# Decoder layer on one core: the feed-forward stage as a written-out pipeline, gate and up in two bank pairs that ScalarE empties

## The reference

```python
def mx_linear(x, w):
    return jnp.einsum('bsh,oh->bso', mx_qdq(x), mx_qdq(w))
g = mx_linear(x, w_gate)
u = mx_linear(x, w_up)
return mx_linear(jax.nn.silu(g) * u, w_down)
...
x = _layernorm(x + _L0_ffn_ref(x, L0_ffn_w_gate, L0_ffn_w_up, L0_ffn_w_down), axis=-1)
```

## Time and profile before

| | |
|---|---|
| median of 3 runs | 887.55 us (886.04 to 888.01) |
| profiled execution | 885.64 us, span 883.8 us |
| busy share of the span | PE 78%, VectorE 73%, ScalarE 59%, POOL 54% |
| granted PE clock, mean | 0.92 of full speed |
| attention pipeline, 300 to 600 us | PE busy 100 of each 100 us, VectorE 83 to 86 |
| feed-forward stage, 750 to 800 us | of 50 us: PE 38.84, VectorE 34.12, ScalarE 15.83, POOL 24.53; clock 0.93 |

### The profile page before, as it was taken

How to read it: one execution, slowest core, us unless ns; L and a number is a source line. 1 busy time by engine, 2 the same in 40 slices (tenths; PEclk the granted TensorE clock), 3 DMA queues, 4 the chain that set the end, 5 groups by cost and what they waited for, 6 DMA issues and landing times.

```text
span 883.8 us, 15272 instructions
## 1 busy us (share of the span) xinstructions
PE 689.3 (78%) x5249; PEld 380.0 (43%) x5264; DVE 642.4 (73%) x1236; ACT 524.6 (59%) x953; POOL 480.7 (54%) x538
## 2 busy tenths in 40 slices
PE   2024665655899999999999999999985787777774
PEld 2013554552345544445444554445552343333331
DVE  4566877775877888888889888898723676667663
ACT  1127878764678777787777877778752233333321
POOL 4223333331647776677766777767653344444452
PEclk9999767676899999999999999999996999999996
DMA  8996101110000000000000000000000000000000
GB/s 197 233 196 216 37 24 36 35 43 1 12 13 1 13 13 14 13 1 13 13 14 13 7 7 13 14 13 1 1 1 0 1 24 24 24 24 24 24 23 26
DMA packets 25829, 30.91 MB, mean 35 GB/s; under 512 B 4016, under 2 KB 16304, under 8 KB 25776
## 3 DMA queue, kind: packets, MB, share of 16 engines
q1 hardware_dynamic: 25776, 30.22, 12.8%
HBM read 26.02 MB, written 4.19 MB: 34 GB/s over the span
## 4 chain that ended last, share of the span: by engine, by line
PE 55%; DVE 11%; POOL 11%; issue 10%; ACT 7%; DMA 4%; ACTq 1%; SPq 1%; POOLq 0%; DVEq 0%
PE banks L1207 7%; PE banks L1168 7%; PE banks L1197 7%; PE banks L1219 7%; PE banks L1178 7%; PE banks L1242 6%; PE banks L1133 6%; ACT big L831 5%; POOL big L544 4%; DVE big L561 4%; POOL rstd L539 3%; DMA big<-in_L_ffn_w_down_dram 2%; DVE big L796 2%; PE banks L1257 2%; DMA big<-in_L_ffn_w_up_dram 2%
## 5 line engine op out<-in xcount | busy, mean ns | idle before, releaser
L831 ACT ACTIVATE big<-banks 128x512 f32<-128x512 f32 (+3 forms) x352 | 197.0, 593 | 73.8 <-PE banks L1197 43.5
L475 POOL TENSOR_TENSOR big<-big 128x512 f32<-128x512 f32 x128 | 131.6, 1049 | 4.3 <-DVE big L697 4.3
L677 DVE TENSOR_REDUCE big<-banks 128x1 f32<-128x512 f32 x128 | 83.0, 681 | 49.7 <-PE banks L1168 48.5
L467 POOL TENSOR_TENSOR big<-big 128x512 f32<-128x512 f32 x64 | 81.2, 1269 | 56.2 <-ACT big L918 56.2
L1133 PE MATMUL banks<-big 128*128 128x128 f32 x256 | 57.8, 417 | 53.7 <-ACT big L831 53.7
L831 ACT ACTIVATE big<-big 32x256 f32<-32x256 f32 (+4 forms) x112 | 90.4, 835 | 1.1
L544 POOL TENSOR_TENSOR big<-big 128x1376 f32<-128x1376 f32 x16 | 40.1, 2508 | 92.4 <-DVE big L565 92.4
L913 ACT ACTIVATE big<-banks,big 128x512 f32<-128x512 f32 x128 | 87.2, 682 | 3.9 <-DVE big L677 3.7
L1047 ACT ACTIVATE big<-big,shift,rstd 128x512 f32<-128x512 f32 x16 | 13.0, 812 | 124.4 <-POOL shift L540 124.4
L683 DVE TENSOR_REDUCE big<-banks 128x16 f32<-128x1024 f32 x64 | 76.6, 1198 | 9.6 <-PE banks L1178 9.6
L918 ACT ACTIVATE big<-big 128x1024 f32<-128x1024 f32 x64 | 67.2, 1050 | 21.9 <-DVE big L688 21.9
(11 more groups left out here) (104 smaller groups left out, 1220.7 us busy)
## 6 DMA issues: line engine op xcount, KB each, us to landing
big<-in_x_dram SPq DMA_DIRECT2D x2, 2048.0 KB, 16.7
big<-in_x_dram SPq DMA_DIRECT2D x4, 1024.0 KB, 10.2
xt<-in_x_dram SPq DMA_DIRECT2D x1, 4096.0 KB, 14.9
big<-in_ctx_dram SPq DMA_DIRECT2D x16, 256.0 KB, 2.8
out_dram<-big SPq DMA_DIRECT2D x16, 256.0 KB, 2.0
big<-in_L_ffn_w_down_dram SPq DMA_DIRECT2D x4, 688.0 KB, 6.9
big<-in_L_ffn_w_gate_dram SPq DMA_DIRECT2D x10, 256.0 KB, 2.6
big<-in_L_ffn_w_up_dram SPq DMA_DIRECT2D x10, 256.0 KB, 2.7
```

The costliest lines, as they stand in the source:

```text
L475: pool.tensor_tensor(e, e, r, ALU.mult).then_inc(s.p_ready, 1)
L677: dve.tensor_reduce(kneg[:, par, i:i + 1], bank[par], X, ALU.max, negate=True).then_inc(s.k_max_ready, 1)
L831: return act.activation(dst, src, ACT.Copy)
```

## The change

The feed-forward stage becomes a pipeline written out tile by tile on every engine, without loops, with more tiles in flight. Gate and up of a chunk go to a pair of banks (0 and 1, or 2 and 3, alternating by chunk). ScalarE empties both: silu of gate into `hs`, which has three slots, and a copy of up into the new `us`, which has two. VectorE multiplies `hs` by `us` in place in one operation of 1376 columns (`multiply_h`), and POOL scales in place too (`shift_hidden`). `hk`, `hq`, `hqT`, `yo`, `xo` and the columns of the output norm have two slots; the down product alternates between banks 6 and 7, in two parts of six and five pieces; all transposes, of x and of h, share banks 4 and 5. Storing uses two semaphores. The last tiles of the attention pipeline are written out, and the first gate and up chunk stands ahead of the last tile's `spread_rn` on PE. The diff, cut:

```diff
...
+        hs = cut(3 * FFN).rearrange("p (s n) -> p s n", s=3)
+        us = cut(2 * FFN).rearrange("p (s n) -> p s n", s=2)
         h8 = cut(FFN // 4).bitcast(FP8)
-        hq = cut(FFN // 2).bitcast(BF16)
-        hqT = cut(FT * P // 2).bitcast(BF16).rearrange("p (f t) -> p f t", f=FT)
-        xqT = cut(L).bitcast(BF16).rearrange("p (s k t) -> p s k t", s=2, k=KT)
-        yo = cut(L)
-        xo = cut(L)
-        hk = [cut(GH) for _ in range(3)]
+        hk = [[cut(GH) for _ in range(3)] for _ in range(2)]
+        assert off <= 4 * NJ * L
+
+        off = 4 * NJ * L
+        hq = cut(FFN).bitcast(BF16).rearrange("p (s n) -> p s n", s=2)
+        hqT = cut(FT * P).bitcast(BF16).rearrange("p (s f t) -> p s f t", s=2, f=FT)
+        yo = cut(2 * L).rearrange("p (s n) -> p s n", s=2)
+        xo = cut(2 * L).rearrange("p (s n) -> p s n", s=2)
...
-            with sp.Fori(0, T) as t:
-                sp.wait_ge(s.out_ready, t + 1)
-                sp.dma_start(out_tok[t], xo).then_inc(s.out_stored, 16)
-            sp.wait_ge(s.out_stored, 16 * T)
+            for u in range(T):
+                sp.wait_ge(s.out_ready, u + 1)
+                sp.dma_start(out_tok[u], xo[:, u % 2]).then_inc(s.out_stored[u % 2], 16)
...
+            def shift_hidden(u):
+                pool.wait_ge(s.h_inv_ready, u + 1)
+                h = hs[:, u % 3]
+                pool.tensor_tensor(groups(h), groups(h), spread(hk[u % 2][1], GH), ALU.mult).then_inc(s.hy_ready, 1)
+
+            def out_rsqrt(u):
+                k = u % 2
+                pool.wait_ge(s.ln_var, u + 1)
+                if u >= 2:
+                    pool.wait_ge(s.out_ready, u - 1)
+                pool.tensor_tensor(neg_mean_o[:, k:k + 1], zero[:], mv_o[:, k, 0:1], ALU.subtract)
+                ch.link(pool.tensor_tensor(vare[:], mv_o[:, k, 1:2], eps_tile[:], ALU.add))
+                ch.link(pool.tensor_tensor(rstd_o[:, k:k + 1], vare[:], minus_half[:, 0:1], ALU.pow))
+                pool.tensor_tensor(shift_o[:, k:k + 1], neg_mean_o[:, k:k + 1], rstd_o[:, k:k + 1], ALU.mult
+                                   ).then_inc(s.ln_shift, 1)
+
+            for f in range(-1, T + 1):
...
+            rsqrt_y(T - 1)
+            add_y(T - 1)
+            x2_rsqrt(T - 1)
+            shift_x(T - 1)
+            for u in range(0, T + 4):
+                if u - 4 in tiles:
+                    out_rsqrt(u - 4)
+                if u in tiles:
+                    shift_hidden(u)
...
+            def multiply_h(u):
+                dve.wait_ge(s.silu_ready, NC * u + NC)
+                dve.wait_ge(s.u_copied, NC * u + NC)
+                dve.tensor_tensor(hs[:, u % 3], hs[:, u % 3], us[:, u % 2], ALU.mult).then_inc(s.h_ready, 1)
+
+            def scale_hidden(u):
+                dve.wait_ge(s.h_ready, u + 1)
+                if u >= 2:
+                    dve.wait_ge(s.hy_ready, u - 1)
+                group_scales(hs[:, u % 3], *hk[u % 2]).then_inc(s.h_inv_ready, 1)
+
+            def clip_hidden(u):
+                dve.wait_ge(s.hy_ready, u + 1)
+                to_fp8(h8, hs[:, u % 3]).then_inc(s.h_clipped, 1)
+
+            def dequant_hidden(u):
+                dve.wait_ge(s.h_clipped, u + 1)
+                if u >= 2:
+                    dve.wait_ge(s.tr_ready, tr_no[u - 2, "h1"] + 1)
+                else:
+                    dve.wait_ge(s.tr_ready, tr_no[T - 1, "p13"] + 1)
+                dve.tensor_tensor(groups(hq[:, u % 2]), groups(h8), spread(hk[u % 2][2], GH), ALU.mult
+                                  ).then_inc(s.hq_ready, 1)
+
+            def add_down(u):
+                dve.wait_ge(s.down_part, 2 * u + 2)
+                if u >= 2:
+                    dve.wait_ge(s.out_ready, u - 1)
+                dve.tensor_tensor(yo[:, u % 2], xt[:, u], bank[6 + u % 2], ALU.add).then_inc(s.down_added, 1)
+
+            def out_stats(u):
+                dve.wait_ge(s.down_added, u + 1)
+                if u >= 2:
+                    dve.wait_ge(s.ln_shift, u - 1)
+                ch.link(dve.bn_stats(st6[:], yo[:, u % 2]))
+                dve.bn_aggr(mv_o[:, u % 2], st6[:]).then_inc(s.ln_var, 1)
...
+            x2_stats(T - 1)
+            scale_x(T - 1)
+            quantize_x(T - 1)
+            for u in range(1, T + 5):
+                if u - 2 in tiles:
+                    scale_hidden(u - 2)
+                if u - 3 in tiles:
+                    clip_hidden(u - 3)
+                    dequant_hidden(u - 3)
+                if u - 5 in tiles:
+                    add_down(u - 5)
+                    out_stats(u - 5)
+                if u - 1 in tiles:
+                    multiply_h(u - 1)
...
+            def silu(u, c):
+                c0, w = CH[c]
+                m = NC * u + c
+                act.wait_ge(s.gu_ready, m + 1)
+                if u >= 3:
+                    act.wait_ge(s.h_clipped, u - 2)
+                act.activation(hs[:, u % 3, c0:c0 + w], bank[2 * (m % 2)][:, 0:w], ACT.Silu).then_inc(s.silu_ready, 1)
+
+            def copy_u(u, c):
+                c0, w = CH[c]
+                m = NC * u + c
+                act.wait_ge(s.gu_ready, m + 1)
+                if u >= 2:
+                    act.wait_ge(s.h_ready, u - 1)
+                copy(us[:, u % 2, c0:c0 + w], bank[2 * (m % 2) + 1][:, 0:w]).then_inc(s.u_copied, 1)
...
+            def result(u):
+                k = u % 2
+                act.wait_ge(s.ln_shift, u + 1)
+                if u >= 2:
+                    act.wait_ge(s.out_stored[k], 16 * (u // 2))
...
+            norm_x2(T - 2)
+            bias_y(T - 1)
+            copy_xT(0)
+            silu(0, 0)
+            copy_u(0, 0)
+            silu(0, 1)
+            copy_u(0, 1)
+            copy_xT(1)
+            silu(0, 2)
+            norm_x2(T - 1)
+            copy_u(0, 2)
+            silu(1, 0)
+            copy_u(1, 0)
+            silu(1, 1)
+            copy_u(1, 1)
+            for u in range(2, T + 6):
+                if u in tiles:
+                    copy_xT(u)
+                if u - 1 in tiles:
+                    silu(u - 1, 2)
+                    copy_u(u - 1, 2)
+                if u - 6 in tiles:
+                    result(u - 6)
+                if u in tiles:
+                    silu(u, 0)
+                    copy_u(u, 0)
+                if u - 3 in tiles:
+                    copy_h(u - 3, 0)
+                if u in tiles:
+                    silu(u, 1)
+                if u - 3 in tiles:
+                    copy_h(u - 3, 1)
+                if u in tiles:
+                    copy_u(u, 1)
...
+            def gate_up(u, c):
+                c0, w = CH[c]
+                m = NC * u + c
+                if c == 0:
+                    pe.wait_ge(s.tr_copied, tr_no[u, "x"] + 1)
+                if m == 0:
+                    pe.wait_ge(s.k_exp_done, 8 * T)
+                elif m == 1:
+                    pe.wait_ge(s.q_shifted, 4 * T)
+                else:
+                    pe.wait_ge(s.silu_ready, m - 1)
+                    pe.wait_ge(s.u_copied, m - 1)
+                for o, wT in ((bank[2 * (m % 2)], wgT), (bank[2 * (m % 2) + 1], wuT)):
+                    for f in range(KT):
+                        last = pe.matmul(o[:, 0:w], xqT[:, u % 2, f], wT[:, f, c0:c0 + w],
+                                         start=(f == 0), stop=(f == KT - 1))
+                last.then_inc(s.gu_ready, 1)
...
+            y_product(T - 1, 0)
+            y_product(T - 1, 1)
+            y_product(T - 1, 2)
+            y_product(T - 1, 3)
+            sum_squares(T - 1)
             transpose_x(0)
             gate_up(0, 0)
+            spread_rn(T - 1)
+            gate_up(0, 1)
             transpose_x(1)
-            turn(1, 1)
-            with pe.Fori(1, T // 2 - 1) as i:
-                for k in range(2):
-                    turn(2 * i + k, k)
-            for k in range(2):
-                turn(T - 2 + k, k)
-            transpose_h(T - 1)
-            down(T - 1)
+            gate_up(0, 2)
+            for u in range(1, T + 4):
+                if u in tiles:
+                    gate_up(u, 0)
+                    gate_up(u, 1)
+                if u - 3 in tiles:
+                    transpose_h(u - 3, 0)
+                    transpose_h(u - 3, 1)
+                if u - 4 in tiles:
+                    down(u - 4, 1)
+                if u + 1 in tiles:
+                    transpose_x(u + 1)
+                if u in tiles:
+                    gate_up(u, 2)
+                if u - 3 in tiles:
+                    down(u - 3, 0)
...
```

More of the change, by code:

```diff
@@ L318, in decoder_kernel @@
         tiles = range(T)
-        transposes = (
+        slot_groups = (
             (1, "ctx"), (1, "k01"), (1, "k10"), (1, "k11"), (1, "k20"), (1, "k21"), (1, "k30"), (1, "p00"),
@@ L323, in decoder_kernel @@
         )
+        middle_groups = (
+            (0, "x"), (1, "x"),
+        )
+        turn_groups = ((3, "h0"), (3, "h1"), (-1, "x"))
         tr_no = {}
```

(35 more changed lines are left out.)

204 lines of the change are left out of this document (56 added, 148 removed).

## The result

| | before | after |
|---|---|---|
| median, same chip, 4 runs each | 887.33 us (886.04 to 888.01) | 851.93 us (849.61 to 853.74) |
| ratio | | 0.9601, 95% interval 0.957 to 0.9633 |
| profiled execution, span | 885.64 us, 883.8 us | 850.38 us, 848.4 us |
| first product to last product of the stage | 684.0 to 860.6 | 683.8 to 823.8 |
| last product to end of span | 23.2 us | 24.6 us |

The change takes 35.4 us off; the forecast was 29.6, with 834 to 874 as the range. The gain lies between the first and the last product, 36.5 us; the end is 1.4 us longer and the start 0.2 to 0.3 earlier.

A forecast was written before the change was run, and what follows sets the result against it. The bound was taken to be the serial POOL and VectorE chain of each tile, 11.76 us. Overlapped turns of 10.02 us, with start and end, gave span 854.2 and, with profiling offsets, 858 us; range 834 to 874.

The forecast's parts named there:

- the likeliest case: Whole kernel: the forecast itself, 858 us against 887.55, with its own range of 851 to 866; chance 0.60.
- The turn: Feed-forward stage: VectorE's steps with neighbouring tiles overlapped sum to 10.02 us per tile against 11.76.
- The port term: VectorE's turn: POOL's waiting scaling goes first when the clip ends, so the dequantisation stands for 2.36 us.
- rival (a): VectorE keeps the port from clip into dequantisation, POOL's scaling runs afterwards: turn 8.44 us, total 836; chance 0.12.
- What POOL does not hold: VectorE steps with an operand in PSUM, or one operand in all, run unhindered beside POOL; the add takes 0.69 us.
- POOL's short steps: POOL's four output steps, 1.27 us, wait behind the product, then fit under the next reduction of 1.59: cost nothing.
- Rival (b): POOL's short steps alternate with VectorE's small scale steps and clip, up to 1.2 us per turn: 875; chance 0.13.
- rival (c): PE, waiting each turn, does part of its work at low clock; at half, turn 13.6 us, total 908; chance 0.06.
- (d): Mixtures between forecast and no change, an in-order wait on ScalarE reaching the product: 866 to 884 us; chance 0.08.
- The start: Lead-in from attention: PE's spread starts near 675.1, and the last tile's quantisation, ahead of the first product, ends near 686.0.
- The early turns: VectorE's first turns of the stage, before the twelve full ones: 5.5, 9.25 and 8.44 us.
- The end: After the last dequantisation at 838.9: transposes, 16 down matmuls at 0.37 each to 847.8, then 6.4 to span 854.2.

The follow-up runs named there:

- A: The kernel after, with POOL's scaling of 22 of the 43 column groups left out (computation incomplete): 831.89 us, ratio 0.9409 to the kernel before.
- B: The kernel after, with VectorE's add and statistics moved ahead of the clip and dequantisation: 844.25 us, ratio 0.9537 to the kernel before.
- D: The kernel after without ScalarE's copy of up; VectorE makes three products straight from PSUM: 897.27 us, ratio 1.0132 to the kernel before.
- G: The kernel after, with small scale steps, add, statistics and next reduction before the clip, last turns in old order: 823.94 us, ratio 0.9307 to the kernel before.
- E: The kernel before plus ScalarE's copy of up and one 1376-wide product, loops and single buffers kept: 914.33 us, ratio 1.0329 to the kernel before.
- C: The kernel after with add and statistics ahead of the clip, except in the last turns, which keep the old order: 838.46 us, ratio 0.9469 to the kernel before.

## Why the prediction was right

Right: forecast 858 us, measured 851.93, just inside the likeliest case's own range (851 to 866): the mechanism was right, and nearly all the small errors of its terms point the same way. Against the profiled execution, forecast 856.0 and found 850.38; the span was 5.8 us too long. By its steps:

- **The turn.** 10.02 forecast, 9.91 found, term by term: scales and clip's start 2.17 (756.07 to 758.24; 2.20), clip 0.90 (0.88), dequantisation with its wait 3.70 (759.14 to 762.84; 2.36 + 1.37 = 3.73), add and statistics 1.54 (1.58), product 1.60 (1.63). Over twelve full turns that is 1.3 us.
- **The port term** was the decisive one, and rival (a), that VectorE keeps the port, is refuted: POOL took over in the 0.03 us between clip and dequantisation in 15 of the 16 tiles (15 x 3.78 + 1.59 = 58.3, the sum of the group; at the last tile POOL has nothing left to scale), and A shows that the wait follows POOL's length one for one. The Trainium skill ("SBUF — State Buffer", section "A bandwidth-pool intuition that's wrong (but worth ruling out)") gives "blocked until DVE-end + ~115 ns" for POOL writing DMA descriptors under a VectorE copy. If it is carried over to a waiting POOL instruction, as in the prediction, the trace disagrees: with 115 ns POOL would have come after the dequantisation. The same page of the Trainium skill, in "Who interferes with whom", says that one side blocks the other fully for a whole instruction and that a reduction never contends. Clip, scaling and dequantisation agree: the dequantisation ends 1.45 us after POOL, its whole 1.59 but for 0.14. So does the reduction: the one at 689.20 takes 1.59 wholly inside POOL's scaling of 687.75 to 691.53. The pow does not, see the last section.
- **What POOL does not hold** was put too widely in the prediction, which counts "one operand in all" as free. The small scale step behind that reduction has one operand and took 0.75 for 0.19 (690.82), until POOL was done, and in B the clip, with one operand too, took 1.87 for 0.87. The sum treated both rightly, so nothing of the forecast hung on it.
- **POOL's short steps** hide as forecast. The first waits behind the product (1.46 for 0.19), the other three run from 756.04 to 757.12, under the reduction, which keeps its 1.59. Rival (b) is refuted in the kernel after; in B the steps were stretched, and still cost nothing, since POOL was the one that waited.
- **PE's clock.** 1.00 from 720 to 780 us, so rival (c) did not occur. No in-order wait on ScalarE reached the product (0.0 us idle before L768), which refutes (d). D shows that (c) was a real danger: with PE waiting longer per turn, the clock fell to 0.89 and 0.91 in two of three windows. The 9.1 us that (c) gave PE per turn was too much: 48.82 of 60 us are 8.1 per turn of 9.91, and G's turn, with PE busy all the time, is 7.86.
- **The start** was 2.2 us too late: first product 683.80 for 686.0. The step that failed is the spread's start at 675.1 with the low clock, 1.98 long. PE's clock rose during the second half of the first chunk (1.78, then 1.51), so the spread began at 673.90 and took 1.09. 0.3 of the 2.2 is that the squares ended earlier in this execution (669.94 for 670.27).
- **The early turns**: 5.40 for 5.5, 8.94 for 9.25, 8.38 for 8.44, and 8.30 for 8.4 at the end, 0.6 us together; the last tile's clip to dequantisation took 0.2 less, since POOL's short step, which waited behind the clip (833.91, 0.73), did not hold the dequantisation up.
- **The end** from the last dequantisation was 13.8 us (834.63 to 848.4) for 15.3. The failed step is 16 down matmuls at 0.37: they took 3.62 in all, 0.23 each, at the high clock. The transposes took 0.6 to the first down matmul for 1.4. Part was given back: they waited behind the down matmuls of the tile before, which ran at 0.41 each, and began 3.2 us after the dequantisation did, not 1.6. The rest, 6.4, came as forecast. 2.2 + 1.3 + 0.6 + 0.2 + 1.5 = 5.8.

The end of the kernel after, in its timeline:

```profile
834.63 1.59 DVE L786 TENSOR_TENSOR big<-big 128x1376 bf16<-128x1376 fp8e4 x1
...
837.79 0.78 PE L1359 MATMUL banks<-ident_bf,big 128*128 128x128 bf16 x11
...
838.41 3.62 PE L1374 MATMUL banks<-wdT,big 128*128 128x512 bf16 x16
```

The prediction read the change as one thing. D and E show that it is two that need each other, which the sum alone did not tell. What raised PE's clock earlier at the seam in one order than in the other was not tried by itself.

## What to carry to other kernels

When VectorE and POOL both work on SBUF, the order within VectorE's turn decides what POOL's operation costs: put what POOL does not hold (here an add with one operand in PSUM, statistics and a reduction, but not the clip and the small scale steps) right behind the step that releases POOL; here that was worth another 26 to 28 us without removing an instruction. An engine that the profile shows as 98% busy may be waiting inside an instruction, so compare each row's length with the same operation alone. And before a ring of PSUM banks is made smaller, ask which engine frees them and what stands ahead of that instruction: freed by VectorE's last step of a turn, the same pipeline was slower than the serial loops.

## What the runs showed that I had not expected

- A waiting POOL operation gets in between two VectorE operations only 0.03 us apart, as the earlier trace rows had suggested once (there POOL had started 0.04 us before the clip ended), and after it has finished, a waiting VectorE operation goes ahead of POOL's next one (B: POOL's step at 759.00 waits behind the clip, the clip behind POOL's scaling).
- The pow is an exception: it does not keep VectorE out for its whole row. In G it starts at 754.66, 0.37 us ahead of the clip, the clip takes its usual 0.87 (755.03 to 755.90), and the pow's row ends only at 755.93, 1.27 for 0.55. In C a pow (821.31, 2.38 us) waits behind the dequantisation and ends only after the clip that follows. What the pow does inside its row, no trace shows.
- How long a POOL row is says little of its work: the 128x1 subtraction lasts 0.19, 0.73, 0.82 or 1.46 us in these traces, by what VectorE holds.
- At the seam, the order with bf16 matmuls first (PE busy from 670.88 on without a gap) had the high clock by about 674 (granted clock 0.53, 0.61 and 1.00 in the 2 us windows from 670, 672 and 674); the order with the fp32 spread first, after 1.74 us of idle, by about 678 (0.50 until 678, then 0.96).
